# A leaky activation written as a linear part and an absolute value, in the second half of layer 2 of a graph network on one core

## What is computed

```python
x = _layernorm(x + _L0_gnn_ref(...)); x = _layernorm(x + _L1_gnn_ref(...))
x = _layernorm(x + _L2_gnn_ref(x, edge_index, ...)); x = _layernorm(x + _L3_gnn_ref(...))

def _gatv2_layer(x, src, dst, Wl, bl, Wr, br, att, bias, heads, out_ch, concat):
    xl = (x @ Wl + bl).reshape(N, heads, out_ch)
    xr = (x @ Wr + br).reshape(N, heads, out_ch)
    e = jax.nn.leaky_relu(xl[src] + xr[dst], NEG_SLOPE)      # NEG_SLOPE = 0.2
    logits = jnp.einsum('ehc,hc->eh', e, att)
    m = jax.ops.segment_max(logits, dst, num_segments=N)
    ex = jnp.exp(logits - m[dst])
    alpha = ex / jax.ops.segment_sum(ex, dst, num_segments=N)[dst]
    out = segment_sum(xl[src] * alpha[..., None], dst)       # mean over the one head
    return out + bias

# L2: src and dst with the loops appended
h = jax.nn.elu(_gatv2_layer(x, ..., Wl1, ..., heads=8, out_ch=16, concat=True))
h = jax.nn.elu(_gatv2_layer(h, ..., Wl2, ..., heads=1, out_ch=64, concat=False))
h = jax.nn.elu(h @ Wlin + blin)
```

## Time and profile before

| | |
|---|---|
| median of 3 runs | 4844.04 us (4839.3 to 4848.83) |
| the profiled execution: its time, its span | 4839.3 us, 4837.6 us |
| busy over the span: PE, PEld, DVE, ACT, POOL | 79%, 53%, 75%, 66%, 64% |
| pass 2b: first DMA start, first of the next pass | 3548.5 us, 4126.3 us |
| mean granted TensorE clock over the span | 0.935 |

### The profile page before, as it was taken

One profiled execution on the slowest core, in us unless ns is written; L12 is line 12 of the kernel. 1 busy time (PEld: TensorE's weight loads), 2 busy tenths in 40 slices (PEclk: granted clock), 3 DMA queues, 4 the chain that ended last, 5 costly groups with the idle time before them and its releaser, 6 DMA issues. The chain is left out here.

```text
span 4837.6 us, 74788 instructions
## 1 busy us (share of the span) xinstructions
PE 3813.0 (79%) x19896; PEld 2560.8 (53%) x20115; DVE 3637.8 (75%) x5894; ACT 3183.7 (66%) x10636; POOL 3089.0 (64%) x3645
## 2 busy tenths in 40 slices
PE   3888888888888699999688886888867777576676
PEld 3666666666666456666465564555534444344444
DVE  3666566666666488888599996999979999577776
ACT  2888888888887578888588885555545555333333
POOL 4889898898998577777444442333234443477775
PEclk9999999999999799999799998999989999788888
DMA  2334334334433333333233332333334433333221
GB/s 68 103 106 109 106 104 112 105 109 111 111 107 95 99 85 94 91 89 82 69 87 88 90 89 63 106 106 107 96 77 107 107 107 89 84 83 83 82 80 48
DMA packets 695838, 451.77 MB, mean 93 GB/s; under 512 B 143539, under 2 KB 623257, under 8 KB 695696
## 3 DMA queue, kind: packets, MB, share of 16 engines
q1 hardware_dynamic: 219504, 182.41, 14.0%
q10 hardware_dynamic: 413392, 186.30, 13.5%
q0 software_dynamic: 62800, 81.68, 7.0%
HBM read 253.00 MB, written 199.90 MB: 94 GB/s over the span
## 5 line engine op out<-in xcount | busy, mean ns | idle before, releaser
L769 POOL TENSOR_TENSOR node_rstd<-node_variance,minus_half 128x4 f32<-128x4 f32 x588 | 650.1, 1109 | 13.5 <-DMA slot_map<-node_value,node_index 1.4
L224 ACT ACTIVATE node_z<-psum 128x128 f32<-128x128 f32 x1960 | 513.5, 277 | 156.7 <-PE psum L204 87.6
L230 DVE TENSOR_TENSOR node_x<-psum,node_rstd 128x512 f32<-128x512 f32 x294 | 202.9, 690 | 487.2 <-POOL node_rstd L769 487.2
L1153 POOL DMA_INDIRECT slot_src_rows<-x,slot_index x392 | 450.8, 1150 | 168.5 <-issue 104.5
L919 POOL DMA_INDIRECT slot_map<-node_value,node_index x392 | 417.6, 1065 | 74.5 <-issue 73.5
L224 ACT ACTIVATION_READ_ACCUMULATOR node_z<-psum 128x1 f32 x1960 | 407.0, 208 | 0.0
L224 ACT ACTIVATE slot_logit<-psum 128x128 f32<-128x128 f32 x980 | 256.7, 280 | 198.0 <-PE psum L204 197.9
L1153 POOL DMA_INDIRECT slot2b_src_rows<-xl,slot2b_index x196 | 249.1, 1271 | 81.8 <-issue 46.2
L213 PE MATMUL psum<-ident,node_x 128*128 128x128 f32 x784 | 140.0, 306 | 193.9 <-DVE node_x L230 193.4
L1139 POOL DMA_INDIRECT out_nodes<-slot_new,slot_side_index x196 | 228.0, 1163 | 91.6 <-POOL slot_side_index L1133 43.8
L204 PE MATMUL psum<-center,slot_t 128*128 128x128 f32 x1176 | 215.1, 285 | 81.5 <-DVE slot_t L1592 52.7
(11 more groups left out here) (400 smaller groups left out, 12778.7 us busy)
## 6 DMA issues: line engine op xcount, KB each, us to landing
x<-node_x ACTq DMA_DIRECT2D x294, 256.0 KB, 2.7
slot_keep<-keep SPq DMA_DIRECT2D x147, 256.0 KB, 3.9
node_xT<-in_x_T SPq DMA_DIRECT2D x98, 256.0 KB, 3.4
out_nodes<-node_x ACTq DMA_DIRECT2D x98, 256.0 KB, 3.0
x<-slot_new ACTq DMA_DIRECT2D x98, 256.0 KB, 2.4
slot_dst_rows<-x SPq DMA_DIRECT2D x98, 256.0 KB, 4.3
staged<-node_gathered ACTq DMA_DIRECT2D x14, 896.0 KB, 5.9
xl<-node_xl ACTq DMA_DIRECT2D x98, 128.0 KB, 3.8
```

Source lines behind the costliest of these rows:

```text
L224: ins = act.activation(g.z[u][:, t, :], rows[:, t, :], ACT.Square, scale=float(D ** -0.5), accum_out=g.mean_square[u][:, t:t + 1])
L230: v.tensor_tensor(out[:, :, :], source, g.rstd[u][:, :].unsqueeze(2).broadcast_to([P, TILES, D]), ALU.mult)\
L769: pool.tensor_tensor(g.rstd[u][:, :], g.variance[u][:, :], g.c.minus_half[:, :], ALU.pow).then_inc(g.pool_out[u], 1)
L1153: pool.indirect_dma_start(src_rows[u][:, t, 0:src_width], None, table, at_index(index[u][:, t:t + 1], 0))\
```

## The change

It rests on leaky(z) = 0.6 z + 0.4 |z| for a slope of 0.2. The linear part of the logit's difference needs no activation: 0.6 att (z_edge - z_loop) is 0.6 att (xl[src] - xl[dst]), a product of `xs` and `xd` with constant matrices. ACT `z` now makes |A + pair_bias|, with `Abs` in place of `Identity` (its row form is otherwise the same). DVE `z` is gone. PE `r` is three products into B instead of one: `straight_src` by `xs`, `straight_dst` by `xd`, and `pair_gap`, now with a factor 0.4, by `t1`. It waits for ACT `z` before the first of them.

The preparation makes the two new matrices: two more loads of a 64-element vector (`bias2_twice`), and seven DVE instructions where there were two. The table of numbers for 2b is new throughout, so all five queues of the pass are in another order.

```diff
-        "2b": (10.65, (10.656, 14.172, 14.895, ...
+        "2b": (10.60, (9.517, 0.000, 0.619, ...
...
     for half in (0, C2):
+        loads.append((bias2_twice[half:half + C2, :], a["L2_gnn_bias2"].rearrange("(p o) -> p o", o=1)))
...
-                                (c.pair_gap[0:C2, :], att2_twice[0:C2, 0:1].broadcast_to([C2, D]))):
...
-            v.tensor_scalar(c.pair_gap[C2:, :], att2_twice[C2:, 0:1].broadcast_to([C2, D]), -1.0, None, ALU.mult).then_inc(worked, 1)
+            for out, half, share in ((c.pair_gap, 0, BENT), (c.pair_gap, 1, -BENT), (c.straight_src, 0, STRAIGHT),
+                                     (c.straight_dst, 0, -STRAIGHT), (c.straight_dst, 1, 0.0)):
+                rows = slice(half * C2, half * C2 + C2)
+                v.tensor_scalar(out[rows, :], att2_twice[rows, 0:1].broadcast_to([C2, D]), share, None, ALU.mult).then_inc(worked, 1)
+            v.scalar_tensor_tensor(out=offset[:, :], in0=bias2_twice[:, :], scalar=1.0, in1=att2_twice[:, :], op0=ALU.add,
+                                   op1=ALU.mult).then_inc(worked, 1)
...
+            v.tensor_scalar(c.straight_src[C2:, :], offset[C2:, 0:1].broadcast_to([C2, D]), -STRAIGHT, None, ALU.mult).then_inc(worked, 1)
...
-        "2b": [("DVE", "dst"), ("PE", "z"), ("ACT", "z"), ("DVE", "z"), ("PE", "r")],
+        "2b": [("DVE", "dst"), ("PE", "z"), ("ACT", "z"), ("PE", "r")],
...
-                    act_copy(act, g, u, t1[u][:, :], A(u), ACT.Identity, (c.blr1 if layer == "2a" else c.pair_bias)[:, 0:1])
+                    if layer == "2a":
+                        act_copy(act, g, u, t1[u][:, :], A(u), ACT.Identity, c.blr1[:, 0:1])
+                    else:
+                        act_copy(act, g, u, t1[u][:, :], A(u), ACT.Abs, c.pair_bias[:, 0:1])
...
                 elif step == "r":
-                    pe.wait_ge(*g.DVE.done(u, i, "z"))
-                    product(u, B, [(c.pair_gap[:, :], first)])
+                    pe.wait_ge(*g.ACT.done(u, i, "z"))
+                    product(u, B, [(c.straight_src[:, :], src), (c.straight_dst[:, :], dst), (c.pair_gap[:, :], first)])
```

More of the change, by code:

```diff
@@ L47 @@
 SLOPE = 0.2
+STRAIGHT, BENT = 0.5 * (1.0 + SLOPE), 0.5 * (1.0 - SLOPE)
 NODE_STREAMS = 7
@@ L335, in prepare @@
     c.pair_src, c.pair_dst, c.pair_gap = sb("pair_src", [P, D]), sb("pair_dst", [P, D]), sb("pair_gap", [P, D])
+    c.straight_src, c.straight_dst = sb("straight_src", [P, D]), sb("straight_dst", [P, D])
     c.Wl2r2, c.Wlin1 = sb("Wl2r2", [P, D]), sb("Wlin1", [C2 + 1, D])
@@ L359, in prepare @@
     raw_blin = load("raw_blin", [P, D], a["L2_gnn_blin"].partition_broadcast(P), room=temp)
-    br2_twice, att2_twice = temp("br2_twice", [P, 1]), temp("att2_twice", [P, 1])
+    br2_twice, att2_twice, bias2_twice = (temp(n, [P, 1]) for n in ("br2_twice", "att2_twice", "bias2_twice"))
+    offset = temp("offset", [P, 1])
     for half in (0, C2):
+        loads.append((bias2_twice[half:half + C2, :], a["L2_gnn_bias2"].rearrange("(p o) -> p o", o=1)))
         loads.append((br2_twice[half:half + C2, :], a["L2_gnn_br2"].rearrange("(p o) -> p o", o=1)))
@@ L475, in _ @@
                                 (c.Wlin1[0:C2, :], c.Wlin[:, :]), (c.pair_src[0:C2, 0:C2], c.ident[0:C2, 0:C2]),
-                                (c.pair_dst[:, 0:C2], c.ident[:, C2:]),
-                                (c.pair_gap[0:C2, :], att2_twice[0:C2, 0:1].broadcast_to([C2, D]))):
+                                (c.pair_dst[:, 0:C2], c.ident[:, C2:])):
                 v.tensor_copy(out, source).then_inc(worked, 1)
             v.tensor_tensor(c.pair_dst[:, C2:], c.ident[:, 0:C2], c.ident[:, C2:], ALU.add).then_inc(worked, 1)
-            v.tensor_scalar(c.pair_gap[C2:, :], att2_twice[C2:, 0:1].broadcast_to([C2, D]), -1.0, None, ALU.mult).then_inc(worked, 1)
+            for out, half, share in ((c.pair_gap, 0, BENT), (c.pair_gap, 1, -BENT), (c.straight_src, 0, STRAIGHT),
[4 more added lines that the diff above has]
+                                   op1=ALU.mult).then_inc(worked, 1)
             v.tensor_tensor(c.self_gap[:, :].rearrange("p (h k) -> p h k", h=4),
@@ L485, in _ @@
             v.tensor_scalar(c.value_bias2[0:C2, :], c.bias2[:, :], 1.0, None, ALU.add).then_inc(worked, 1)
-            setup += 10
+            setup += 14
             to_center = ((raw["W1a"], c.W1a), (raw["W1b"], c.W1b), (raw["W2"], c.W2), (c.W, c.Wc),
@@ L502, in _ @@
             v.tensor_scalar(c.value_bias1[:, :], c.node_bias1[:, :], 1.0, None, ALU.add).then_inc(worked, 1)
+            v.tensor_scalar(c.straight_src[C2:, :], offset[C2:, 0:1].broadcast_to([C2, D]), -STRAIGHT, None, ALU.mult).then_inc(worked, 1)
             v.tensor_copy(c.pair_bias[C2:, :], br2_twice[C2:, :]).then_inc(worked, 1)
             v.tensor_tensor(c.pair_bias[0:C2, :], br2_twice[0:C2, :], c.value_bias2[0:C2, :], ALU.subtract).then_inc(worked, 1)
-            n += 14
+            n += 15
             v.wait_ge(products, 1)
@@ L584, in _ @@
             pe.wait_ge(made, 30)
-            pe.wait_ge(worked, 25)
+            pe.wait_ge(worked, 29)
             pe.matmul(psum[:, 6, 0:D], all_ones[:, :], c.Wl2r2[:, :], start=True, stop=True)
@@ L588, in _ @@
             pe.transpose(psum[:, 0, 0:D], c.W[:, :], c.ident[:, :]).then_inc(products, 1)
-            pe.wait_ge(worked, 25 + 7 + 14 + 3 + 10 + 5 * 8 + 1)
+            pe.wait_ge(worked, 29 + 7 + 15 + 3 + 10 + 5 * 8 + 1)
             for b, lhs, rhs, m in ((1, WT, S["att_src"], D), (2, WT, S["att_dst"], D), (3, raw["Wn"], S["a_src"], D),
```

## The result

The changed kernel takes 4811.4 us, median of four runs (4804.0 to 4814.6). The kernel before, beside it, takes 4843.0 us (4839.3 to 4848.8). The ratio is 0.9932, with 0.9916 to 0.9948 as its interval of 95%: 32 us saved, where 29 were predicted. The profiled execution has a span of 4802.3 us, that of before 4837.6, so 35 us less.

A forecast was written before the change was run, and what follows sets the result against it. VectorE was taken to bound pass 2b. Rounds -41.9, stalls +4, run-in +3.0, drain +3.8 and preparation +2.2 summed to -28.9 us: 4844.0 to 4815 us, with an 8-in-10 range of 4806 to 4836.

The forecast's parts named there:

- 48 undisturbed rounds: Pass 2b: VectorE loses the leaky step, so a round falls from 10.81 to 10.1 us (ends 10.06 and 10.21).
- stalls: Pass 2b: 4 us of VectorE waits left, where 8 to 11 are now, since a fuller TensorE should keep its clock.
- run-in of 2b: Start of 2b: two more slow products before the first `f`, +3.7, less the leaky step's 0.7: +3.0 us.
- drain of 2b: End of 2b: `rB` of the last chunk behind the slow `y2` of the chunk before, two 1.91 us groups: +3.8 us.
- preparation: Before the passes: two more vector loads and seven small VectorE instructions for two, 2.2 us at most.
- the other new neighbours have nothing between them that isn't there already: VectorE's new queue in 2b: apart from `rec` between `f` and `shift`, which gives nothing, other new adjacencies change nothing.
- The wait of TensorE ahead of `srcT`: 2b's changed profile: TensorE's only wait, about 1 us a round, released by `x3`.
- the range of 485 to 490: 2b's changed profile: the 49 scans `f` take 485 to 490 us (10.1 to 10.2 a round) instead of 526.7.
- first rival: 2b: pace gained but TensorE's clock falls as often as now, 13 to 20 us of stalls, 4824 to 4831 us; 14%.
- second: 2b: TensorE takes VectorE's place as bound, round stays 10.8 us, 4849 us, or 4835 for half of it; 13%.
- third: 2b: chain `x3` to `h4` at 1.2 GHz makes rounds of 11.6 us, 4883 us, two thirds about 4860; 5%.
- fourth: ScalarE in 2b: `Abs` needs a table load, then another for `exps`, 1.28 us each; 4859 us; 2%.

## Why the prediction was right, step by step

| term, us | predicted | measured |
|---|---|---|
| 48 undisturbed rounds | -34.1 (10.81 to 10.1) | -25.9 (10.76 to 10.22) |
| stalls | -3.8 (7.8 to 4) | -11.9 (10.2 to -1.7) |
| run-in of 2b | +3.0 | -0.3 |
| drain of 2b | +3.8 | +3.9 |
| preparation | +2.2 | +2.1 |
| sum | -28.9 | -32.1 |
| profiled span, median of runs | | -35.3, -31.6 |

The 3.2 us between the sum and the span lie in passes that the change doesn't touch: 0 and 1 together took 3.9 us less in this one execution, the last pass 0.5 more. The mechanism came as predicted, but that the sum fits to 3 us is luck: the round came 8.2 us short, the stalls and the run-in 8.1 and 3.3 us better than forecast.

**The round was mis-sized.** VectorE gave 0.54 us and not the 0.71 of the forecast. I compare the starts of 17 rounds after with 13 undisturbed ones before. The leaky step gives 0.60, as said. `sv` to its next neighbour fell from 0.754 to 0.642 us, 0.11 and not 0.15, because that neighbour is now `h4`, not `ns`, and it doesn't reach the usual 0.60. And the sentence that "the other new neighbours have nothing between them that isn't there already" failed; it also says that `last` and `x3` stay adjacent, where the old queue has `fc` between them. The three short instructions cost 0.31 us in the old round (0.093 `rec`, 0.050 `last`, 0.165 `fc`) and cost 0.45 in the new one (0.162, 0.229, 0.062). Before, they stood together; in the timeline of the kernel before:

```profile
4074.62 0.18 DVE L1584 RECIPROCAL slot2b_recip<-psum 128x4 f32<-128x4 f32 x1
4074.71 0.13 DVE L1612 TENSOR_TENSOR slot2b_rstd<-slot2b_raw,last 128x4 f32<-128x4 f32 x1
4074.76 0.15 DVE L1504 COPY slot2b_fmax<-slot2b_fmax 128x1 f32<-128x1 f32 x1
4074.95 0.69 DVE L1623 TENSOR_TENSOR slot2b_new<-psum,slot2b_rstd 128x512 f32<-128x512 f32 x1
```

Now each stands alone between two long ones, `last` right ahead of the `x3` that reads it (3909.84 to 3910.09). -0.60 - 0.11 + 0.14 is -0.57, and the measured difference is -0.54. These are distances read from the two traces; why they are what they are isn't shown, and moving `last` won only 0.04 us. That the round before was 10.76 in the mean and not 10.81 (they alternate, 10.69 and 10.81, and the earlier trace rows show a long one) is worth 2.4 us of the term, and as much of the stalls.

**The stalls were mis-sized the other way.** I left 4 us and there are none: the pass is 1.7 us under 48 x 10.22, because its first and last rounds are short (9.52 and 9.15 us). Before, it was 10.2 over 48 x 10.76. The direction was argued rightly, from pass 2a, and the experiment with the idle products shows the cause on its own: more TensorE work, nothing else, and the clock stands at 1.00 and the waits of VectorE are gone. The Trainium skill (TensorE: Matmul & The Clock Gate, What's actually happening) has activity as what releases the throttle. By it the forecast would have had no stalls, and in the changed kernel trace and page agree. The step from "more products" to "no falls" was not safe for all that: the same products in the old order left the clock at 0.95.

**The run-in** was charged +3.0 us and gave 0.3 back. The working doubled the prices of the three products of `r` at 1.2 GHz. In the changed kernel only the products of the first `z` run at the slow level:

```profile
3562.36 2.04 PE L1319 MATMUL psum<-slot2b_xs,pair_src 128*128 128x512 f32 x2 [1.57 <-DVE slot2b_fmax L1516]
...
3566.63 1.13 PE L1319 MATMUL psum<-slot2b_xs,straight_src 128*128 128x512 f32 x2
...
3567.59 1.02 PE L1319 MATMUL psum<-slot2b_xd,straight_dst 128*128 128x512 f32 x2
...
3568.45 1.02 PE L1319 MATMUL psum<-slot2b_t,pair_gap 128*128 128x512 f32 x2
```

The kernel before has at this place:

```profile
3569.29 2.08 PE L1307 MATMUL psum<-slot2b_t,pair_gap 128*128 128x512 f32 x2 [1.50 <-DVE slot2b_t L1502]
```

Before, TensorE stood still for 1.50 us ahead of `r` and was still slow; after, it works through from 3562.36 on and is fast when `r` comes. From the start of `r` to `f` it is 3.0 us now (3566.63 to 3569.6) and was 2.2 (3569.29 to 3571.48), and the leaky step's 0.7 us ahead of `r` is gone: nearly nothing in sum. The first `f` starts 22.7 us after the pass's first load, 23.0 before. The products are not free here, though; the order pays for them. In the new order with the old formula:

```profile
3572.05 2.05 PE L1304 MATMUL psum<-slot2b_xs,pair_src 128*128 128x512 f32 x2 [1.57 <-DVE slot2b_xd L1484]
...
3576.94 1.12 PE L1304 MATMUL psum<-slot2b_t,pair_gap 128*128 128x512 f32 x2 [0.63 <-DVE slot2b_fmax L1501]
...
3578.18 1.28 DVE L1514 TENSOR_TENSOR_SCAN slot2b_fmax<-slot2b_keep,slot2b_fmax,psum 128x512 f32<-128x512 f32 x1
```

From the first product of `z` to `f` this is 6.1 us. The kernel before takes 7.4, the changed kernel 7.2, and the new formula in the old order 9.6. So the new formula costs 2.2 us in the old order and 1.1 in the new one, and the new order, in which the next stream's transposes follow `z` and TensorE is fast when `r` comes, gives back 1.3. The working had left that out. The time ahead of `z` is that of the loads and differs between chips: the changed kernel's first `f` comes after 22.7 us on one and after 30.4 on another.

**The drain** came as worked out. From the last `f` to the next pass's first load it is 32.0 us, before 28.1. TensorE of the changed kernel as the pass drains, and the wait of VectorE behind it:

```profile
4069.45 1.91 PE L1448 MATMUL psum<-slot2b_x_rows,ident 128*128 128x512 f32 x2
...
4071.16 1.91 PE L1450 MATMUL psum<-center,slot2b_t 128*128 128x128 f32 x8
...
4072.86 1.06 PE L1416 MATMUL psum<-ident,slot2b_recip 128*128 128x128 f32 x4
4074.03 0.68 DVE L1604 TENSOR_TENSOR slot2b_t<-slot2b_t,psum 64x512 f32<-64x512 f32 x1 [4.16 <-PE psum L1416]
```

`rB` (L1416) of the last chunk stands behind the two slow groups of `y2`, one shown as 1.91 us in the earlier trace rows, now both, and `agg` waits 4.16 us for it. On the other chip the changed kernel's drain is 32.1 us.

**The preparation** moved the start of the first pass by 2.1 us (64.9 to 67.0), with the two loads and the five small instructions as priced.

**The signs and rivals.** The wait of TensorE ahead of `srcT`, 1.00 us in 44 rounds, its 90%, VectorE's 98% and the clock were there as written; the scans stand over 488.9 us, in the range of 485 to 490, for the two reasons above and not for the one given. The clock falling as often as before (first rival) is refuted by the clock of 1.00. TensorE as the bound (second) is refuted by two runs: one instruction more on VectorE costs 26 us, one product more in `z` leaves the rounds as they are. Slower by a chain at 1.2 GHz (third) didn't come, but its mechanism is real and near: 0.86 us more in that chain turn the gain of 0.6% into no gain. In the old order, where the formula costs 68 us, the slower rounds do come with a lower clock, 0.95. A table load for `Abs` (fourth) isn't there; the page counts the same 200 and 194 loads in both kernels, two of them in 2b, and here the trace agrees with the Trainium skill (ScalarE: Activation LUTs, Table sets).

## What to carry to other kernels

Where one engine is full, work moved off it may pay only if the order moves with it: here the formula alone lost 68 us, the order alone 8, and both together gained 32. Price a removed step by the distance between starts, and price its new neighbours as well: here three short instructions took 0.31 us in a row and 0.45 one by one. Work added to an engine with gaps is judged by its place on the chains between engines, not by that engine's busy time.

## What was not expected of the hardware

- TensorE work that computes nothing made the kernel before faster. Two idle products a round raised its clock from 0.97 to 1.00 and took 9.4 us out of the 49 scans. Two useful ones in the old order, on the path to `f`, went with a clock of 0.95.
- A VectorE instruction of 0.13 to 0.18 us costs from 0.05 us (behind another short one) to 0.25 us (alone, ahead of the one that reads it) of the queue; alone between two that don't read it, 0.06 to 0.19.
- TensorE was 98% busy with 0.15 us of waiting a round and held no round up.
- In the run-in, where TensorE works without a wait since its first product, a product takes 1.13 us at 19.7 us into the pass; in the kernel before, after a wait of 1.50 us, one took 2.08 us at 20.8 us.
